# Dividing the attention weights before they are split, and P times V in four column tiles

## What is computed

```python
x = x + xattn(layernorm(x), ctx)     # x, ctx: 16 x 128 rows of 1024
# q = xn @ w_q.T (32 heads of 32); k, v = ctx @ w_k.T, ctx @ w_v.T (8 groups of 32, four heads share one)
# scores = q k^T / sqrt(32), masked (128 x 128 in each sequence); P = softmax(scores)
# attn = P v, then @ w_out.T
x = x + ffn(layernorm(x))            # w3(silu(x1) * x2) + b3, x1 and x2 from w12
```

## Time and profile before

| | |
|---|---|
| three timed runs, us | 1040.89, 1041.44, 1043.1 (median 1041.44) |
| span of the profiled execution, us | 1040.4 |
| PE busy | 1017.7 us (98%) |
| DVE busy | 661.6 us (64%) |
| POOL busy | 498.6 us (48%) |
| ACT busy | 447.3 us (43%) |
| granted TensorE clock, mean | 0.998 |

### The profile page before, as it was taken

One profiled execution on the slowest core, in us unless ns is written; L12 is line 12 of the kernel. 1 busy time (PEld: TensorE's weight loads), 2 busy tenths in 40 slices (PEclk: granted clock), 3 DMA queues, 4 the chain that ended last, 5 costly groups with the idle time before them and its releaser, 6 DMA issues.

```text
span 1040.4 us, 21876 instructions
## 1 busy us (share of the span) xinstructions
PE 1017.7 (98%) x8400; PEld 695.6 (67%) x8400; DVE 661.6 (64%) x2080; ACT 447.3 (43%) x983; POOL 498.6 (48%) x476
## 2 busy tenths in 40 slices
PE   7897999999999999999999999999999999999998
PEld 6786868869687696886655544444444888468853
DVE  6789977767787777888646234636864447625431
ACT  6768556557465574664766210123431112202100
POOL 2869923727337273379958596158742301212000
PEclk9999999999999999999999999999999999999999
DMA  9669686998989999789946715494758631974201
GB/s 367 227 160 197 168 216 168 222 247 222 248 211 229 230 245 244 179 236 232 268 94 123 253 71 203 94 345 160 272 200 185 235 112 40 236 230 122 83 31 51
DMA packets 230776, 199.12 MB, mean 191 GB/s; under 512 B 177040, under 2 KB 187280, under 8 KB 225808
## 3 DMA queue, kind: packets, MB, share of 16 engines
q1 hardware_dynamic: 230672, 197.72, 69.0%
HBM read 119.04 MB, written 35.65 MB: 149 GB/s over the span
## 4 chain that ended last, share of the span: by engine, by line
PE 87%; DVE 6%; DMA 1%; ACT 1%; issue 0%; SPq 0%; DVEq 0%
PE bank_dense L1349 52%; PE bank_spare L1349 13%; PE bank_score L1494 6%; PE bank_spare L1494 6%; PE bank_av L1494 3%; PE bank_score L1406 2%; DVE arena_attn L1820 2%; DVE arena_attn L1830 1%; PE bank_av L1424 1%; PE bank_av L1428 1%; PE bank_av L1426 1%; PE bank_dense L1366 1%; DMA k_scratch<-arena_in 1%; PE bank_spare L1358 0%; PE bank_dense L1358 0%
## 5 line engine op out<-in xcount | busy, mean ns | idle before, releaser
L1153 ACT ACTIVATE arena_attn<-arena_attn,arena_in 128x128 f32<-128x128 f32 x512 | 162.7, 391 | 94.6 <-DVE arena_in L1820 93.6
L1349 PE MATMUL bank_dense<-arena_rows,arena_in 128*128 128x256 f16 (+1 forms) x1272 | 175.2, 295 | 1.9 <-POOL arena_in L874 1.0
L936 POOL TENSOR_TENSOR arena_attn<-arena_attn 128x512 f16<-128x512 f32 x89 | 102.6, 1170 | 148.8 <-ACT arena_attn L1160 148.8
L1349 PE MATMUL bank_dense<-arena_attn,arena_rows 128*128 128x512 f16 x768 | 166.4, 379 | 0.0
L1349 PEld LDWEIGHTS bank_dense<-arena_rows,arena_in 128*128 128x128 f16 x1272 | 123.0, 98 | 43.1 <-DVE arena_in L1668 1.6
L1820 DVE CUSTOM_DVE_ANT_0 arena_attn<-bank_score,arena_in 128x128 f32<-128x128 f32 x512 | 143.5, 346 | 0.4 <-PE bank_score L1406 0.4
L1349 PEld LDWEIGHTS bank_dense<-arena_attn,arena_rows 128*128 128x128 f16 x768 | 75.2, 98 | 90.2
L1349 PE MATMUL bank_dense<-arena_out,arena_attn 128*128 128x512 f16 x576 | 127.8, 379 | 0.0
L1349 PEld LDWEIGHTS bank_dense<-arena_out,arena_attn 128*128 128x128 f16 x576 | 55.5, 98 | 63.3
L1349 PE MATMUL bank_spare<-arena_rows,arena_in 128*128 128x256 f16 (+1 forms) x648 | 87.6, 292 | 0.0
L1349 PE MATMUL bank_dense<-arena_out,arena_in 128*128 128x512 f16 x384 | 83.0, 379 | 0.0
(11 more groups left out here) (219 smaller groups left out, 1890.8 us busy)
## 6 DMA issues: line engine op xcount, KB each, us to landing
arena_rows<-x SPq DMA_DIRECT2D x32, 512.0 KB, 6.1
arena_in<-w_scratch SPq DMA_DIRECT2D x64, 256.0 KB, 3.1
arena_attn<-q_scratch SPq DMA_DIRECT2D x48, 256.0 KB, 4.5
arena_rows<-w_t SPq DMA_DIRECT2D x12, 1024.0 KB, 6.2
arena_rows<-ctx_t SPq DMA_DIRECT2D x8, 1024.0 KB, 6.1
q_scratch<-arena_attn SPq DMA_DIRECT2D x16, 512.0 KB, 5.1
x_scratch<-arena_rows SPq DMA_DIRECT2D x16, 512.0 KB, 3.8
arena_out<-x_scratch SPq DMA_DIRECT2D x16, 512.0 KB, 5.9
```

The lines of the kernel that those rows point to most:

```text
L936: ins = pool.tensor_tensor(p_split[:, g % 2, u, 1], e[:, g % 2, u], p_split[:, g % 2, u, 0], ALU.subtract)
L1153: ins = act.activation(head, head, ACT.Exp, bias=neg_max[:, g % 2, h:h + 1], scale=-1.0)
L1349: ins = pe.matmul(dst, lhs(a, c), rhs(b, c), start=(c == chunks[0] and n == 0), stop=(c == chunks[-1] and n == 2))
```

## The change

For groups 8 to 47 (stages 2 to 6) P is divided by its row sum before it is split. ACT's `Exp` also accumulates the row sums. DVE gets two new pieces of work, `norm_prob(g, 0)` behind `attn_lo(g-3)` in step `g`, and `norm_prob(g, 1)` at the very start of step `g+1`. Each takes the reciprocals of four sums and multiplies 128x512 of `e` by them, in place, and by 2^14. The reciprocals lie in PSUM, save for groups 8 and 9, where they lie in SBUF. `prob_hi(g)` waits for both halves. `divide` and `turn_attn` go for these groups. `weigh(g-3)` takes the place of `turn_attn(g-3)`. In it V is the stationary operand (32 columns, in the column tile of head j), and transposed P streams, 128 columns: 24 products that give the transposed result in bank "a". The factor 2^-14 goes into `attn_hi` and `attn_lo`. SP's `turn_prob(g)` now waits for `weigh(g-2)` in its new place. `scale_rows` is put ahead of `prob_hi`. The function `by_pool` is always false, so that POOL gets no division.

```diff
+NORMED = range(8, 48)
+P_SCALE = 2.0 ** 14
+        p_sum = part(arena_attn, 59, 1, F32)[:, 0:2 * U * HPG].rearrange("p (r u j) -> p r u j", r=2, u=U)
+        inv_first = part(arena_attn, 61, 1, F32)[:, 0:2 * U * HPG].rearrange("p (r u j) -> p r u j", r=2, u=U)
+        inv_bank = B_AV[:, 0:2 * U * HPG].rearrange("p (r u j) -> p r u j", r=2, u=U)
+        def weighed(g):
+            return (s_dense, done("a", g)) if g in NORMED else (s_av, divided_count(g))
...
 def turn_prob(g):                                   # SP
                 if g >= 2:
-                    sp.wait_ge(s_av, g - 1)
+                    sp.wait_ge(*weighed(g - 2))
...
 def attn_hi(g):                                     # ACT
-                act.activation(attn_t[:, g % RING, 0], bank("a", g)[:, 0:AB], ACT.Copy).then_inc(s_dhi, 1)
+                act.activation(attn_t[:, g % RING, 0], bank("a", g)[:, 0:AB], ACT.Copy,
+                               scale=1 / P_SCALE if g in NORMED else 1.0).then_inc(s_dhi, 1)
 def exps(g, u):
+                    if g in NORMED:
+                        ins = act.activation(head, head, ACT.Exp, bias=neg_max[:, g % 2, h:h + 1], scale=-1.0,
+                                             accum_out=p_sum[:, g % 2, u, j:j + 1])
 def prob_hi(g):
+                if g in NORMED:
+                    act.wait_ge(s_vnorm, vector_count(g, 1))
...
                     unit_hi(second_unit(t, s))
-                    prob_hi(g)
                     if t < NB - 1 and s in (4, 6):
                         scale_rows(2 * t + s // 2)
+                    prob_hi(g)
...
 def weigh(g):                                       # PE
+                if g in NORMED:
+                    dst = begin("a", g)
+                    terms_of_out = ((v_high, 0), (v_low, 0), (v_high, 1))
+                    for u in range(U):
+                        for n, (v, piece) in enumerate(terms_of_out):
+                            for j in range(HPG):
+                                ins = pe.matmul(dst[DH * j:DH * j + DH, SEQ * u:SEQ * u + SEQ],
+                                                v[:, a % 2, u, m, 0:DH], prob_t[:, g % 2, u, piece, j],
+                                                start=n == 0, stop=n == 2, tile_position=(0, DH * j))
+                    ins.then_inc(s_dense, 1)
+                    return
...
-                    if g >= 3:
+                    if g >= 3 and g - 3 in NORMED:
+                        weigh(g - 3)
+                    elif g >= 3:
                         turn_attn(g - 3)
...
-                    if g >= 2:
+                    if g >= 2 and g - 2 not in NORMED:
                         weigh(g - 2)
...
+            def norm_prob(g, u):                    # DVE
+                sums_inv = (inv_first if g < NORMED[2] else inv_bank)[:, g % 2, u]
+                dve.wait_ge(s_exp, 2 * g + u + 1)
+                dve.reciprocal(sums_inv, p_sum[:, g % 2, u]).then_inc(s_rec, 1)
+                dve.wait_ge(s_rec, half_count(g, u))
...
+                heads = e[:, g % 2, u].rearrange("p (j n) -> p j n", j=HPG)
+                dve.scalar_tensor_tensor(out=heads, in0=heads, scalar=P_SCALE,
+                                         in1=sums_inv.rearrange("p (j o) -> p j o", o=1).broadcast_to([P, HPG, SEQ]),
+                                         op0=ALU.mult, op1=ALU.mult).then_inc(s_vnorm, 1)
 def divide(g):
+                if g in NORMED:
+                    return
 def attn_lo(g):
+                if g in NORMED:
+                    dve.scalar_tensor_tensor(out=attn_t[:, g % RING, 1], in0=bank("a", g)[:, 0:AB], scalar=1 / P_SCALE,
+                                             in1=attn_t[:, g % RING, 0], op0=ALU.mult, op1=ALU.subtract).then_inc(s_dread, 1)
+                    return
...
+                    if g - 1 in NORMED:
+                        norm_prob(g - 1, 1)
                     if g >= 3:
                         divide(g - 3)
                     mask_scores(g)
...
                     if g >= 3:
                         attn_lo(g - 3)
+                    if g in NORMED:
+                        norm_prob(g, 0)
```

More of the change, by code:

```diff
@@ L302, in later_unit, with by_pool, normed_count, half_count @@
     return UNITS * (f - PLAIN) + i
+def by_pool(g):
+    return False
+def normed_count(g, kind=lambda n: n in NORMED):
+    return sum(kind(n) for n in range(g + 1))
+def half_count(g, u):
+    return U * normed_count(g - 1) + u + 1
+def vector_count(g, u):
+    return half_count(g, u) - normed_count(g, by_pool)
+def divided_count(g):
+    return g + 1 - normed_count(g)
 def plo_count(g):
@@ L409, in xattn_ffn @@
         kept, with_6, with_5, with_7 = [terms[:, 0], terms[:, 1]], terms[:, 2], terms[:, 3], terms[:, 4]
+        p_sum = part(arena_attn, 59, 1, F32)[:, 0:2 * U * HPG].rearrange("p (r u j) -> p r u j", r=2, u=U)
+        inv = part(arena_attn, 60, 1, F32)[:, 0:HPG]
+        inv_first = part(arena_attn, 61, 1, F32)[:, 0:2 * U * HPG].rearrange("p (r u j) -> p r u j", r=2, u=U)
         k_stack = part(arena_attn, 63, 4).rearrange("p (b g n) -> p b g n", b=2, g=4)
@@ L559, in xattn_ffn @@
         s_av, s_inv, s_avread = sem("av_done"), sem("inv_sum_done"), sem("attn_ready")
+        s_pnorm, s_vnorm = sem("prob_normed_by_pool"), sem("prob_normed_by_vector")
+        s_rec, s_vinv = sem("inv_sum_of_prob_done"), sem("inv_sum_for_pool_done")
         s_scales, s_cout = sem("block_scales_done"), sem("c_out_done")
@@ L810, in _ @@
             for k in range(2, 4):
-                sp.wait_ge(s_av, NG)
+                sp.wait_ge(*weighed(NG - 1))
                 sp.dma_start(w3_in[k], w3_t[k]).then_inc(s_w3load[k], 16)
@@ L937, in prob_lo, with norm_prob @@
                 ins.then_inc(s_plo2, 1)
+            def norm_prob(g):
+                pool.wait_ge(s_vinv, normed_count(g, by_pool))
+                heads = e[:, g % 2, 0].rearrange("p (j n) -> p j n", j=HPG)
+                pool.tensor_tensor(heads, heads, inv.rearrange("p (j o) -> p j o", o=1).broadcast_to([P, HPG, SEQ]),
+                                   ALU.mult).then_inc(s_pnorm, 1)
             halves = range(2), range(2, 4)
@@ L941, in _ @@
                 for s in range(STEPS):
-                    if GROUPS * (t - 1) + s > PLO_ALONE:
-                        prob_lo(GROUPS * (t - 1) + s - 1)
+                    g = GROUPS * (t - 1) + s
+                    if g > PLO_ALONE:
+                        prob_lo(g - 1)
+                    if by_pool(g):
+                        norm_prob(g)
                     if t < NB and s in (0, 1):
@@ L1141, in v_hi @@
                 if u == 0 and t >= 2:
-                    act.wait_ge(s_av, GROUPS * (t - 1))
+                    act.wait_ge(*weighed(GROUPS * (t - 1) - 1))
                 act.wait_ge(s_dense, done("v", t, u))
@@ L1152, in exps @@
                     head = e[:, g % 2, u, SEQ * j:SEQ * j + SEQ]
-                    ins = act.activation(head, head, ACT.Exp, bias=neg_max[:, g % 2, h:h + 1], scale=-1.0)
+                    if g in NORMED:
+                        ins = act.activation(head, head, ACT.Exp, bias=neg_max[:, g % 2, h:h + 1], scale=-1.0,
+                                             accum_out=p_sum[:, g % 2, u, j:j + 1])
+                    else:
+                        ins = act.activation(head, head, ACT.Exp, bias=neg_max[:, g % 2, h:h + 1], scale=-1.0)
                 ins.then_inc(s_exp, 1)
             def prob_hi(g):
-                act.wait_ge(s_exp, 2 * g + 2)
+                if g in NORMED:
+                    act.wait_ge(s_vnorm, vector_count(g, 1))
+                    if by_pool(g):
+                        act.wait_ge(s_pnorm, normed_count(g, by_pool))
+                else:
+                    act.wait_ge(s_exp, 2 * g + 2)
                 if g >= 2:
@@ L1362, in turn_attn @@
             def turn_attn(g):
-                pe.wait_ge(s_avread, g + 1)
+                pe.wait_ge(s_avread, divided_count(g))
                 dst = begin("a", g)
@@ L1416, in weigh @@
                     pe.wait_ge(s_dread, done("v", a, 1))
-                if g:
-                    pe.wait_ge(s_avread, g)
-                else:
+                if g == 0:
                     pe.wait_ge(*taken("ctx1"))
+                if divided_count(g - 1):
+                    pe.wait_ge(s_avread, divided_count(g - 1))
+                if g in NORMED:
[9 more added lines that the diff above has]
+                    return
                 for u in range(U):
@@ L1831, in prob_lo @@
                    .then_inc(s_plo, 1)
+            def norm_prob(g, u):
[3 more added lines that the diff above has]
+                dve.wait_ge(s_rec, half_count(g, u))
+                if u == 0 and by_pool(g):
+                    dve.tensor_scalar(inv, sums_inv, P_SCALE, None, ALU.mult).then_inc(s_vinv, 1)
+                    return
[3 more added lines that the diff above has]
+                                         op0=ALU.mult, op1=ALU.mult).then_inc(s_vnorm, 1)
             def divide(g):
```

(6 more changed lines are left out.)

3 lines of the change are left out of this document (2 added, 1 removed).

## The result

The kernel after takes 1059.35 us (median of 4 runs, 1058.65 to 1060.63), the kernel before, run on the same chip, 1042.09 (4 runs). The ratio is 1.0171, 95% interval 1.0156 to 1.0185: slower by 17 us, where the forecast was 8. The profiled execution's span is 1056.5 us, 16.1 more than before.

A forecast was written before the change was run, and what follows sets the result against it. PE was taken as the bound, busy 324.85 of 325.52 us in stages 2 to 6. The terms -4.8 + 3.0 + 1.0 + 8.8 = +8.0 us gave a span of 1048.4, told as a median of 1049 us, range 1034 to 1064.

The forecast's parts named there:

- the chain behind it: Stages 3 to 6: the later division delays `prob_hi`, POOL, the transpose and the weight load behind it; DVE waits 3.3 us.
- step 7 of stages 3 to 6: Late DVE work makes PE wait 2.2 us in step 7 of each of four stages, +8.8 us in all.
- M: Time from PE's start of a step to DVE's first mask; for step 7 put at 2.2 us, 3.4 with late loads.
- PE, 40 groups: Groups 8 to 47: new `weigh` at 0.70 us replaces 0.82 of old work, saving 0.12 a group, 4.8 us.
- stage 2, steps 0 to 6: Steps 1 to 3, where DVE has no idle time: PE waits once for masks behind new halves, +3.0 us.
- step 7 of stage 2: PE waits about 1.0 us for DVE in this step, with M at 2.2: +1.0 us.
- rival C: New `weigh`: tiles do not overlap, 1.32 us or more each; slower, 1065 us in all; chance 0.15.
- the pace of the old pairs: Old `weigh`: a weight load and product pair every 0.025 us, so 0.60 for the new one's 24 pairs.
- Rival A: New `weigh`: tiles overlap better than the old pace, 0.33 to 0.45 us each; faster, 1037 us; chance 0.22.
- the ends: Passing between full array and tiles around `weigh`: 0.10 us for both ends together, bounds 0 and 0.30.
- PE's wait = (M - 1.0) + 0.4 - 0.15 - 0.5: Step 7 of each stage: later M plus ACT's 0.4, less 0.15 bank cover and 0.5 from the longer `weigh`.
- Rival B: DVE's new work stays covered, only 3.5 us of waits remain; faster, 1036 us; chance 0.13.

The follow-up runs named there:

- e7: Kernel after with e1's loads first, groups 12 to 47 only, and step 5's weight load not waiting for the maximum of ctx: 1042.24 us, ratio to before 0.9993.
- e1: Kernel after with SP issuing the ctx and weight loads ahead of the transpose in step 3 of stages 3 to 6: 1048.85 us, ratio to before 1.0034.
- e6: Kernel after with groups 12 to 47 changed instead of 8 to 47: 1056.84 us, ratio to before 1.0140.
- e5: Kernel after with 20 extra unused transposes on PE ahead of `weigh` in step 7 of stages 3 to 5: 1055.06 us, ratio to before 1.0117.
- e2: Kernel after without any division of P for groups 8 to 47, row sums and tiles kept: 1033.51 us, ratio to before 0.9902.
- e9: e7 with ACT's and DVE's pieces that free PE's banks put first in step 7 of stages 2 to 6: 1036.42 us, ratio to before 0.9946.
- e3: Kernel after with DVE's division written to an unused buffer and `prob_hi` not waiting for it: 1048.71 us, ratio to before 1.0047.
- e4: Kernel after with the products of `weigh` ordered by head, three in a row per column tile: 1061.15 us, ratio to before 1.0165.
- e8: e7 with DVE masking before it makes the second half of the division in step 7: 1059.02 us, ratio to before 1.0151.

## Why the prediction was right or wrong

It named the side, the place and the chain behind it, and the size came out at 17 us instead of 8. The step that failed is the term for step 7 of stages 3 to 6: 8.8 us forecast, 17.9 measured. Its M was put at 3.4 and is up to 5.06, and what the clock costs behind a wait, 1.6 to 1.7 us each in stages 3 to 5, was not in the sum at all. By the prediction's own steps, on the profiled executions:

| term | predicted | measured |
|---|---|---|
| PE, 40 groups | -4.8 | -10.8 |
| stage 2, steps 0 to 6 | +3.0 | +4.5 |
| step 7 of stage 2 | +1.0 | +0.8 |
| step 7 of stages 3 to 6 | +8.8 | +17.9 |
| not in the sum | 0 | +3.7 |
| sum | +8.0 | +16.1 |

The measured terms are differences of the step lengths with 0.27 added back for each group that the step weighs. That the sum is off by no more than 8.1 is partly luck: the terms that were too small miss by 14.3 together, and PE's saving, too small as well, gives 6.0 of it back.

*PE.* `weigh` was taken as 0.60 + 0.10 and is 0.46 + 0.09. The upper bound of 1.62 and with it rival C fall: 24 starts spread over four tiles pass in six groups, 0.056 each, and the pace of the old pairs, 0.025, was no limit here. Rival A had that part right, its 4 ns between tiles too (3 to 4 here), but at 0.55 the change saves 0.27 and not up to 0.49. The Trainium skill, "TensorEngine Tiling (Array Packing)", Key Properties, says that a change of mode drains the engine. This trace shows 0.09 us more ahead of `weigh`, and 0.16 instead of 0.056 between its last four and the next unit, 0.10 more: about 0.1 at each end, where 0.15 was my bound and 0.10 for both ends together my choice. So two inputs were off against each other, the pace (0.60 taken, 0.35 measured) and the ends (0.10 taken, 0.2 measured).

*Step 7: the formula held, M and the clock did not.* The prediction had PE's wait = (M - 1.0) + 0.4 - 0.15 - 0.5, that is M - 1.25. For M = 1.78, 2.92, 4.48, 5.01 and 5.06 (stages 2, 6, 3, 5, 4) it gives 0.53, 1.67, 3.23, 3.76 and 3.81. The trace has 0.46, 1.55, 3.12, 3.56 and 3.61. That it fits so well is in part luck. The 0.15 in it is the cover of the bank that DVE's low piece of x frees for the last unit of v, and that unit never waits. PE stands ahead of the second transposes of x, first for the read in `gather_top` (L1689), then for the low piece of v (L1861); all of these stand behind the masks in DVE's list, and so move with M. Two inputs were mis-sized:

- M. Without late loads it was put at 2.2 and is 2.40 (e7). With them it was put at 3.4, and is 4.48 to 5.06 in stages 3 to 5, 2.92 in stage 6. The load comes about as late as forecast: DVE waits 2.56, 3.70, 4.04 and 1.52 us for it (3.3 predicted), in stage 4 until 12.1 into the step (11.1 predicted). But the text let steps 5 and 6 win back 1.3 each. Step 5 did so, the first mask of stage 4 coming 6.62 into step 5 and 5.34 into step 6. Step 6 won 0.28, since DVE waited once more, 0.80, for the load behind. I had named that load and sized it too small. e1 shows the chain's worth.
- The clock. Of the 17.9 us, 11.8 are waits (3.12, 3.61, 3.56, 1.55), 6.1 are what comes on top, 2.0 in each of stages 3 to 5. Of these 2.0 some 0.35 are not the clock but the part of a break that the brackets leave out: step 7 of e7 has it too, 9.96 - 8.57 with waits of 1.04, all at 1.00. The clock is the other 1.6 to 1.7 a stage, 5 us in all. The unit of v alone is 1.67 longer, e6's stage 3 is 1.63 shorter behind the same waits at 1.00, and e5 shows by experiment that the fall comes of PE's standing still: three filled steps of three kept 1.00, though by e6's stage 3 one of them might have kept it anyway. The sum had no term for what a wait of PE costs after its end.

*Stage 2.* The place was right, the work that ends the wait was not. I had DVE's masks of groups 9 and 10 let PE wait; in the trace it is `divide` of group 5 that comes too late for its turn (2.17 us), and step 4 adds another 1.24. The slow clock behind the 2.17 cost nothing here: steps 1 and 2 take 10.45 + 5.99 = 16.44 us, and in e1, where the clock stayed at 1.00, 8.91 + 7.52 = 16.43. DVE sets the pace there, and PE only waits less afterwards (in e1 1.39 us more, ahead of the next turn). The long division of 1471 ns, foreseen as 0.5 more for a half, was one of four. e6 takes stage 2 back to 64.59.

*Not in the sum.* 1.5 lie mostly in step 4 of stage 6 and step 5 of stages 4 and 5; 2.2 outside the five stages. No experiment was spent on the latter. 0.6 are the start: the first scores of stage 2 come that much later than in the trace before. 0.6 are only moved: stage 2 has the new `weigh` of five groups (8 to 12) and is rid of the old one of six (8 to 13), and stage 7 has the old one of group 48 and the new one of group 47 in one step (6.86 us instead of 6.51), so that the 4.5 of stage 2 are really 5.1. The other 1.0 lie in steps 3 and 7 of stage 7 (11.63 instead of 10.87, 9.41 instead of 9.12).

*DVE and ACT.* A half costs 0.21 + 0.61 = 0.82 us to the next instruction (0.84 predicted). Rival B, that DVE's work stays covered, falls: e2 takes 26 us from the kernel after, far more than the 3.5 that B allowed. How much of it is order and not load, e9 shows, which has the division on the same engine in all but four of the 40 groups and stands 3 us (by the ratios 4.6) above e2.

What stays open is when the clock falls. In step 7 of stages 2 to 6, over the profiles of the kernel after and of e1, e3, e4, e5, e6 and e8, and leaving out the steps that e5 filled, it stayed at 1.00 behind all waits that sum to 1.91 us or less, and fell behind 16 of the 19 that sum to 2.21 or more; the other three are 3.14 (e6, stage 3), 2.89 (e8, stage 4) and 2.25 (e5, stage 6). In stage 2 the same wait of 2.17 us for `divide` took it to 0.50 in the kernel after and left it at 1.00 in e1. In stage 1 a wait of 3.27 us of the kernel before left it at 1.00, and at the same place one of 3.12 us in e7 and one of 3.38 us in e9 were followed by 0.50.

## What to carry to other kernels

On an engine that is 98% busy a wait has to be priced twice: by its length and by the granted clock of what follows, here 1.6 to 1.7 us behind a wait of 3, unless another engine sets the pace there anyway. When work goes onto an engine ahead of something that another queue waits for, follow that queue to its end: the step that cost most was a weight load standing behind a transpose, and moving it gave back 10 to 14 of 17 us for nothing. And a change that loses may hold a gain: leave out its costly half first (e2), to see what order of the rest is worth looking for.

## What the runs showed of the hardware

*Tiles work out of program order, as far as the records tell.* e4's products come in another order than the program's and take the same 0.46 to 0.47 us. The Trainium skill, "TensorE: Matmul & The Clock Gate", Part 3 (The mechanism), has products start strictly in program order. The records of e4 don't agree: the program's second product is the first with `v_low`, and it starts at 258.389, behind four with `v_high` that start from 258.323 to 258.353. Its weight loads do begin in a changed order, so the products were not put back in the old order before they ran. That each tile takes up its own products as it comes free would fit the starts; it is my reading of them, and that the records give the starts in the array rightly to 0.01 us isn't shown. The time of 0.47 is measured either way.

*Two inputs in SBUF on DVE meet POOL.* In stage 2 the first division of group 8 took 1.47 us and its second, over as many numbers, 0.69. Timelines of DVE and POOL:

```profile
119.67 1.47 DVE L1913 SCALAR_TENSOR_TENSOR arena_attn<-arena_attn 128x512 f32<-128x512 f32 x1
123.04 0.69 DVE L1913 SCALAR_TENSOR_TENSOR arena_attn<-arena_attn 128x512 f32<-128x512 f32 x1
...
119.43 1.16 POOL L913 TENSOR_TENSOR arena_in<-arena_in 128x512 f16<-128x512 f32 x1
...
123.13 1.61 POOL L913 TENSOR_TENSOR arena_in<-arena_in 128x512 f16<-128x512 f32 x1
```

The first began 0.24 us behind POOL's operation and ended 0.55 behind its end. The second began 0.09 ahead of POOL's, kept its 0.69, and POOL's took 1.61 instead of 1.16. In these two meetings whoever came second waited. With the small operand in PSUM all 76 took 686 to 689 ns, whatever POOL did.
